# The expert bias moves from TensorE's accumulation to VectorE's residual rows

## The chip, the cores and the metric

The kernel runs on one core of a Trainium2 chip. The metric is the device time of one execution in microseconds (us); three runs of the kernel before gave 578.5, 578.75 and 578.78, a median of 578.75. The core has five engines that run side by side, each with its own queue of instructions, and that wait for each other through semaphores: TensorE (PE: matrix products; its weight loads are told apart as PEld), VectorE (DVE), ScalarE (ACT), GpSimd (POOL) and SyncE (SP, which issues most of the DMAs).

## The reference

Two layers of attention and feed-forward over 32 batches of 128 tokens with 128 features. The change concerns the last part, a mixture of eight experts, of which each token takes the one with the highest gate:

```
    indices_s = jnp.argmax(gates, axis=1)
    scores = jnp.max(gates, axis=1)
    for e in range(E):
        mask = (indices_s == e).astype(x.dtype)[:, None]
        h = jax.nn.gelu(x @ w1[e] + b1[e], approximate=False)
        out = out + mask * (h @ w2[e] + b2[e])
    out = out * scores[:, None]
    ...
    x = x + _L1_ffn_ref(_layernorm(x, axis=-1), ...)
```

So a token's row of the result is x + score * (h @ w2[e] + b2[e]), with x the residual row, and score and e those of the token.

## The kernel before

The kernel goes through its stages in order: the first attention (to about 200 us), the feed-forward layer in pairs of batches (from about 202 us, with the second attention beginning in its later pairs), the second attention (to about 474 us), and the expert stage (to about 569 us, then the last write-outs).

During the second attention, each token's normalised row, its residual row, its score and its number are scattered to a table in memory, sorted by expert. The expert stage takes 39 blocks of 128 rows from this table, each of a single expert. Three sets of buffers (`TURNS = 3`) go round. `block_loop` unrolls the first steps (block numbers up to 5), runs the next 30 in a loop of five passes with six steps each, in which the block number j is a register, and unrolls the last three. Each engine has its own copy of that loop. For block j:

- SyncE (lines 469 to 480) reads the block's first row number from memory into a register and issues two loads: XA, the normalised rows (once the buffer's previous rows are transposed), and XB, the residual rows with score and number (once the buffer's previous block has its result, `b_y_ready`).
- VectorE (lines 1743 to 1758) reads the number of the expert of block j+2 into a register (`value_load`, line 1748) and with it picks that expert's b1 (line 1749, b1e) and w1 (line 1750, W1e). Then, for block j, it waits for XB and for the buffer's last write-out, copies the row numbers (line 1754), waits for the product (`b_down`) and computes `by` = product * score + XB (line 1757).
- TensorE (lines 837 to 869) transposes XA of block j+2 (line 845), multiplies block j+1 by w1 (line 854: four products, eight matmul records), reads the expert of block j (line 860), and accumulates for block j first b2 and then h @ w2 (line 866: eight records). The b2 product at line 862 is a 16-bit matmul: `thrice`, a matrix with ones in rows 0, 32 and 64 and zeros elsewhere, against `bpieces`, which holds in those rows b2 cut into three bf16 pieces.
- ScalarE copies the transposed rows (line 1097) and applies gelu with b1 as its bias (line 1102).
- GpSimd writes `by` out, row by row, by the numbers (line 1337).

The pieces of b2 are made by VectorE in the first seven pairs of the feed-forward stage (lines 1706 to 1740, called by the pair's number from `biases`): four memsets for `thrice`, then copies and subtractions on `bpieces` and M2b, ten instructions. M2b, b2 of all experts repeated over 96 partitions, is loaded at about 190 us.

The order on each engine is that of the program; there is no planner. A wait on a semaphore stands either in the instruction that follows or in an entry of its own on the engine's sequencer, which also does the register operations.

Of the kernel before, what the change touches and what calls it, by code (L numbers as in the profile page):

```python
# [8 lines left out]
ALU = mybir.AluOpType  # L9
# [3 lines left out]
BF16 = mybir.dt.bfloat16  # L13
# [7 lines left out]
FC = FF // 128  # L21
# [39 lines left out]
def build(nc, a, out):  # L61
    ctx = ExitStack()
    with ctx:
# [10 lines left out]
        def count(value):  # L74
# [50 lines left out]
        wgr = sb("wgr", [EXPERTS, GATE])  # L125
        M1 = sb("M1", [128, EXPERTS, FF])
        M2 = sb("M2", [128, EXPERTS, FC, 128])
        M2b = sb("M2b", [96, EXPERTS, 128])
        rank = sb("rank", [128, EXPERTS])


# [48 lines left out]
        XB = [sb(f"XB{i}", [128, RW - D])[:] for i in range(TURNS)]  # L180
        bxT = [sb(f"bxT{i}", [128, 128])[:] for i in range(TURNS)]
        by = [sb(f"by{i}", [128, D + 1])[:] for i in range(TURNS)]
        bpieces = sb("bpieces", [96, EXPERTS, 128], BF16)
        b1e = [sb(f"b1e{i}", [128, FC])[:] for i in range(TURNS)]
        thrice = sb("thrice", [96, 128], BF16)
        wgT = sb("wgT", [GATE, EXPERTS])
        wgn = sb("wgn", [EXPERTS, 3])
        wgs = sb("wgs", [EXPERTS, 2, GATE])
# [53 lines left out]
        late_loads = [(F1[:], a["F1"]), (F2[:], a["F2"].rearrange("(c p) n -> p c n", p=128))]  # L242
        expert_loads = [
            (M1b[:], a["M1b"]),
            (M2b[:].rearrange("p e n -> p (e n)"), a["M2b"].rearrange("e n -> (e n)").partition_broadcast(96)),
            (M1[:], a["M1"].rearrange("e p n -> p e n")),
            (M2[:], a["M2"].rearrange("e (c p) n -> p e c n", p=128)),
        ]
# [254 lines left out]
        def _(pe):  # L503
# [334 lines left out]
            def experts():  # L838
                def step(j, r, turn):
                    n1, n2 = (r + 1) % TURNS, (r + 2) % TURNS  # L840
                    if not isinstance(j, int) or j + 2 < BLOCKS:

                        pe.wait_ge(sem(f"xa_loaded{n2}"), 16 * (turn + (r + 2) // TURNS))
                        pe.wait_ge(sem("b_xT_ready"), count(j + 2))
                        nc.tensor.transpose(bank[0][:, 0:128], XA[n2], eye[:]).then_inc(sem("b_transposed"), 1)
                    if not isinstance(j, int) or 0 <= j + 1 < BLOCKS:


                        if isinstance(j, int) and j + 2 >= BLOCKS:
                            pe.wait_ge(sem("b_xT_ready"), j + 2)  # L850

                        pe.wait_ge(sem("b_picked"), count(j + 2))
                        for c in range(FC):
                            mm = nc.tensor.matmul(bank[1 + n1][:, c * 128:(c + 1) * 128], W1e[n1][:, c * 128:(c + 1) * 128], bxT[n1],  # L854
                                                  start=True, stop=True)
                        mm.then_inc(sem("b_up"), 1)
                    if not isinstance(j, int) or 0 <= j < BLOCKS:


                        e = pe.value_load(expert[0:1, bass.ds(j, 1)], min_val=0, max_val=EXPERTS - 1)  # L860
                        pe.wait_ge(sem("b_y_ready"), count(j + 1 - TURNS))
                        nc.tensor.matmul(bank[4 + r][:, 0:D], thrice[:], bpieces[:, bass.ds(e, 1), :].rearrange("p o n -> p (o n)"),
                                         start=True, stop=False)
                        pe.wait_ge(sem("b_gelu"), count(j + 1))
                        for c in range(FC):
                            mm = nc.tensor.matmul(bank[4 + r][:, 0:D], bhT[r][:, c * 128:(c + 1) * 128],  # L866
                                                  M2[:, bass.ds(e, 1), c:c + 1, :].rearrange("p o c n -> p (o c n)"),
                                                  start=False, stop=(c == FC - 1))
                        mm.then_inc(sem("b_down"), 1)

                pe.wait_ge(sem("biases_cut"), 1)
                block_loop(pe, step, -2, BLOCKS)

            step = attention(0)
# [471 lines left out]
        def _(dve):  # L1346
# [260 lines left out]

                return step

            def ffn(early, biases):  # L1610
                def x_of(p):
                    if isinstance(p, int):
                        return lambda i: X[:, 2 * p + i, :]
                    return lambda i: X[:, bass.ds(p * 2 + i, 1), :].rearrange("p o d -> p (o d)")

                def stats_of(p, b):
                    if is_pair(p):
                        norm_stats("f_xn_ready", p, 2, x_of(p), fstats[:, b], fmv[:, b])

                def normalise(p, b):  # L1620
                    if is_pair(p):

                        dve.wait_ge(sem("f_transposed"), count(p - 1))
                        norm_apply("f_xn_ready", p, 2, x_of(p), fmv[:, b], frstd[:, b], lambda i: fxn[:, b, i, :])

                def add(p):

                    dve.wait_ge(sem("f_biased"), p + 1)
                    for h in range(2):
                        dve.wait_ge(sem("f_down"), 2 * p + h + 1)  # L1630
                        x = x_of(p)(h)
                        nc.vector.tensor_tensor(x, x, bank[(4, 7)[h]][:, 0:128], ALU.add).then_inc(sem("f_added"), 1)

                def x_stats(p):

                    dve.wait_ge(sem("f_added"), 2 * p + 2)
                    for t in range(2 * p, 2 * p + 2):
                        nc.vector.bn_stats(xst[:, t, :], X[:, t, :]).then_inc(sem("x1_stats"), 1)
                    dve.wait_ge(sem("x1_stats"), 4 * p + 2)
                    for t in range(2 * p, 2 * p + 2):  # L1640
                        nc.vector.bn_aggr(xmv[:, t, :], xst[:, t, :]).then_inc(sem("x1_stats"), 1)

                def step(p, b):
                    stats_of(p + 4, b)
                    normalise(p + 3, 1 - b)
                    if p in biases:
                        biases[p]()
                    add(p)
                    x_stats(p)
                    run_early(early, p)  # L1650

                def begin(p):

                    dve.wait_ge(sem("attn_added"), 2 * p + 2)
                    stats_of(p, p % 2)
                    if p:
                        normalise(p - 1, (p - 1) % 2)

                def rest():
                    dve.wait_ge(sem("attn_added"), B)  # L1660
                    every_pair(step)
                    dve.wait_ge(sem("f_added"), 2 * PAIRS)

                return begin, rest
# [38 lines left out]
                dve.wait_ge(sem("placing"), 13)  # L1703
                nc.vector.tensor_scalar(base[:], place[:, 2, :], float(EXPERTS * REGION), None, ALU.add).then_inc(sem("expert_ready"), 1)

            def bias_ones():

                nc.vector.memset(thrice[:], 0.0).then_inc(sem("bias_cut"), 1)
                dve.wait_ge(sem("bias_cut"), 1)
                for k in range(3):  # L1710
                    nc.vector.memset(thrice[32 * k:32 * k + 1, :], 1.0).then_inc(sem("bias_cut"), 1)

            def bias_first():

                dve.wait_ge(sem("experts_loaded"), EXPERTS_LOADED)
                nc.vector.tensor_copy(bpieces[:], M2b[:]).then_inc(sem("bias_cut"), 1)

            def bias_rest():

                dve.wait_ge(sem("bias_cut"), 5)  # L1720
                nc.vector.tensor_tensor(M2b[:], M2b[:], bpieces[:], ALU.subtract).then_inc(sem("bias_cut"), 1)

            def bias_second():

                dve.wait_ge(sem("bias_cut"), 6)
                nc.vector.tensor_copy(bpieces[32:64], M2b[32:64]).then_inc(sem("bias_cut"), 1)

            def bias_again():

                nc.vector.tensor_copy(bpieces[64:96], M2b[64:96]).then_inc(sem("bias_cut"), 1)  # L1730

            def bias_last():

                dve.wait_ge(sem("bias_cut"), 8)
                nc.vector.tensor_tensor(M2b[64:96], M2b[64:96], bpieces[64:96], ALU.subtract).then_inc(sem("bias_cut"), 1)

            def bias_third():

                dve.wait_ge(sem("bias_cut"), 9)
                nc.vector.tensor_copy(bpieces[64:96], M2b[64:96]).then_inc(sem("biases_cut"), 1)  # L1740

            def experts():
                def step(j, r, turn):
                    n2 = (r + 2) % TURNS
# [6 lines left out]
                    if not isinstance(j, int) or 0 <= j < BLOCKS:  # L1751
                        dve.wait_ge(sem(f"xb_loaded{r}"), 16 * turn)
                        dve.wait_ge(sem(f"gone_out{r}"), count(16 * (turn - 1)))
                        nc.vector.tensor_copy(by[r].bitcast(I32)[:, D:D + 1], XB[r].bitcast(I32)[:, TOKEN_AT - D:TOKEN_AT - D + 1]
                                              ).then_inc(sem("b_numbered"), 1)
                        dve.wait_ge(sem("b_down"), count(j + 1))
                        nc.vector.scalar_tensor_tensor(by[r][:, 0:D], bank[4 + r][:, 0:D], XB[r][:, SCORE_AT - D:SCORE_AT - D + 1],  # L1757
                                                       XB[r][:, 0:D], ALU.mult, ALU.add).then_inc(sem("b_y_ready"), 1)
# [112 lines left out]
            def regions_set():  # L1871
# [3 lines left out]
                nc.vector.tensor_scalar(sums[:, 0, :], rank[:], float(REGION // 128), None, ALU.mult).then_inc(sem("regions_set"), 1)  # L1875

            early = attention(1)
            begin, every = ffn(early, {0: bias_ones, 1: bias_first, 2: bias_rest, 3: bias_second, 4: bias_again, 5: bias_last,
                                      6: bias_third})
            body_loop(dve, step, START, {-3: partial(x_group, 2),  # L1880
                                         B - 8: gate_square, B - 7: mean_abs, B - 6: gate_unit, B - 5: gate_turned,
                                         B - 4: gate_plain, B - 3: gate_centred, B - 2: scale_norm, B - 1: fold_bias,
# [93 lines left out]
```

## Time and profile before

| | |
|---|---|
| median of three runs | 578.75 us |
| the three runs, lowest to highest | 578.5 to 578.78 us |
| the profiled execution: its own time is its span | 578.6 us |
| busy over the span: PE / PEld / DVE / ACT / POOL | 85 / 63 / 69 / 62 / 64% |
| expert stage, first `by` to last `by` | 491.1 to 568.9 us |
| granted clock of TensorE, mean | 0.964 |

The span runs from the first to the last instruction of one execution. Busy time counts instructions at work on an engine's data path; register operations, branches and semaphore waits of its sequencer are not counted. A letter q behind an engine's name marks such entries of its queue. "issue" as the cause of idle time means that the engine waited for nothing that the profile shows. Matmuls are pipelined, so the length of one is longer than the distance from one to the next.

### The profile page before, as it was taken

How to read it: one execution, taken by the hardware profiler on the slowest of the kernel's cores; microseconds unless marked ns; L12 is line 12 of the kernel's file. 1: busy time of each engine (PE TensorE's matmuls, PEld its weight loads, DVE VectorE, ACT ScalarE, POOL GpSimd, SP SyncE). 2: the span in 40 equal slices, each digit the busy share in tenths (PEclk: the TensorE clock that was granted, in tenths of full speed). 3: DMA queues.
4: the chain of work that ended last, by engine and by line, in shares of the span. 5: the costliest groups of instructions: out<-in, count | busy, mean ns of one | idle time of the engine just before them, and what ended most of it. 6: DMA issues, size and time to landing. Idle time of an engine off the chain costs nothing.

```text
span 578.6 us, 20130 instructions
## 1 busy us (share of the span) xinstructions
PE 493.0 (85%) x6238; PEld 361.9 (63%) x6239; DVE 399.0 (69%) x1248; ACT 357.1 (62%) x872; POOL 372.8 (64%) x755
## 2 busy tenths in 40 slices
PE   3587899999997799988999999999998834999993
PEld 2455666666665599976455555555554423999992
DVE  6687777777888578645578888888888762444441
ACT  4356677777766555653566776777765643666661
POOL 6868766676772367676556688888885561455552
PEclk9879999999999999999899999999999965999997
DMA  6664353534332860004433545444543114333330
GB/s 170 159 135 110 88 131 81 127 88 114 104 76 56 265 156 1 2 19 126 110 91 94 127 128 143 106 111 130 146 121 93 36 68 134 94 91 98 101 87 27
DMA packets 102161, 59.92 MB, mean 104 GB/s; under 512 B 20338, under 2 KB 98178, under 8 KB 102098
## 3 DMA queue, kind: packets, MB, share of 16 engines
q1 hardware_dynamic: 98738, 51.79, 35.5%
q0 software_dynamic: 2784, 6.82, 3.4%
q8 instruction: 32, 0.52, 0.4%
q10 hardware_dynamic: 576, 0.53, 0.3%
q14 instruction: 31, 0.25, 0.2%
HBM read 19.90 MB, written 8.81 MB: 50 GB/s over the span
## 4 chain that ended last, share of the span: by engine, by line
PE 47%; DVE 14%; issue 13%; SPq 8%; DMA 7%; POOL 5%; ACT 4%; ACTq 1%; DVEq 0%; POOLq 0%
DVE negmax L1448 6%; PE bank L688 6%; PE score L632 4%; PE bank L802 4%; PE scoreT L792 4%; DMA stack<-pieces 3%; PE bank L866 3%; PE bank L575 3%; PE bank L544 3%; SPq L404 3%; PE bank L703 2%; PE scoreT L854 2%; PE scoreT L661 2%; PE score L601 2%; SPq L470 2%
## 5 line engine op out<-in xcount | busy, mean ns | idle before, releaser
L1448 DVE TENSOR_REDUCE negmax<-score 128x8 f32<-128x1024 f32 x128 | 156.2, 1220 | 29.9 <-PE score L632 20.1
L975 ACT ACTIVATE P<-scoreT 128x1024 f32<-128x1024 f32 x128 | 131.0, 1024 | 40.1 <-PE scoreT L652 20.3
L688 PE MATMUL bank<-P,Vc 128*32 128x128 f32 x2048 | 82.7, 279 | 2.3 <-DVE product L1556 1.2
L632 PE MATMUL score<-stack 64*128 64x128 bf16 x1024 | 62.3, 221 | 15.6 <-DVE negmax L1448 9.5
L1337 POOL DMA_INDIRECT out<-by x39 | 40.2, 1031 | 51.3 <-issue 26.8
L632 PEld LDWEIGHTS score<-stack 64*128 64x128 bf16 x1024 | 33.6, 95 | 42.0 <-issue 23.1
L688 PEld LDWEIGHTS bank<-P,Vc 128*32 128x32 f32 x2048 | 48.6, 109 | 16.4 <-issue 4.3
L981 ACT COPY outs<-bank 128x256 f32<-128x256 f32 x64 | 23.7, 370 | 49.2 <-PE bank L688 49.2
L1199 POOL TENSOR_TENSOR pieces<-full,pieces 128x256 bf16<-128x256 f32 x63 | 42.2, 670 | 12.8 <-ACT pieces L956 12.8
L1202 POOL TENSOR_TENSOR pieces<-rest,pieces 128x256 bf16<-128x256 f32 x63 | 43.7, 693 | 4.9
L866 PE MATMUL bank<-M,bhT 128*128 x312 | 43.5, 282 | 0.3 <-ACT bhT L1102 0.3
L1200 POOL TENSOR_TENSOR rest<-full,pieces 128x256 f32<-128x256 f32 x63 | 42.4, 673 | 0.0
L1102 ACT ACTIVATE bhT<-scoreT,b1e 128x128 f32<-128x128 f32 x104 | 29.6, 368 | 15.9 <-PE scoreT L854 14.6
L1210 POOL TENSOR_TENSOR negp<-negmax,blank 128x16 bf16<-128x16 f32 x64 | 14.3, 223 | 38.4 <-DVE negmax L1448 36.9
L866 PEld LDWEIGHTS bank<-M,bhT 128*128 128x128 f32 x312 | 37.9, 192 | 1.3 <-issue 0.7
L1256 POOL DMA_INDIRECT expert_rows<-XR,sloti x32 | 32.9, 1027 | 8.8 <-issue 6.7
L1188 POOL TENSOR_TENSOR full<-rotA,rotB 128x256 f32<-128x256 f32 x31 | 22.5, 727 | 22.4 <-DVE rotB L1400 22.4
L1757 DVE SCALAR_TENSOR_TENSOR by<-bank,XB 128x128 f32<-128x128 f32 x39 | 13.7, 351 | 27.7 <-PE bank L866 20.3
L1457 DVE RECIPROCAL rden<-bank 128x16 f32<-128x16 f32 x64 | 16.2, 254 | 23.9 <-PE bank L703 23.7
L802 PEld LDWEIGHTS bank<-F,hT 128*128 128x128 f32 x256 | 31.0, 192 | 0.8
L802 PE MATMUL bank<-F,hT 128*128 128x128 f32 x256 | 31.2, 275 | 0.0
L1013 ACT ACTIVATE xn<-XR,xsh,xrs 128x128 f32 (+1 forms) x64 | 28.0, 487 | 5.2 <-POOL xsh L1162 5.1
(219 smaller groups left out, 1261.7 us busy)
## 6 DMA issues: line engine op xcount, KB each, us to landing
stack<-pieces SPq DMA_DIRECT2D x192, 128.0 KB, 2.5
ctxT<-in_ctxT SPq DMA_DIRECT2D x32, 128.0 KB, 2.4
XB<-expert_rows SPq DMA_DIRECT2D x39, 66.0 KB
XA<-expert_rows SPq DMA_DIRECT2D x39, 64.0 KB
XR<-in_x SPq DMA_DIRECT2D x4, 512.0 KB, 4.3
stack<-blank SPq DMA_DIRECT2D x32, 64.0 KB, 2.1
stack<-negpT SPq DMA_DIRECT2D x64, 32.0 KB, 1.9
M<-in_M SPq DMA_DIRECT2D x1, 2048.0 KB, 9.8
```

Of the source, the lines that this page charges most:

```text
L632: mm = nc.tensor.matmul(SCORE[:, r, i * 128:(i + 1) * 128], Qs[pb][rows, h, tb * S:(tb + 1) * S], Ks[pb][rows, kv, tb * S:(tb + 1) * S], s ...
L688: mm = nc.tensor.matmul(PVOUT[VCOL * i:VCOL * (i + 1), half * 128:(half + 1) * 128], Vc[:, k % BODY, at:at + VCOL], P32[:, c, i * 128:(i + ...
L802: mm = nc.tensor.matmul(bank[(4, 7)[h]][:, 0:128], hT[:, b, c, h * S:(h + 1) * S], F2[:, c, :], start=(c == 0), stop=(c == FC - 1))
L866: mm = nc.tensor.matmul(bank[4 + r][:, 0:D], bhT[r][:, c * 128:(c + 1) * 128], M2[:, bass.ds(e, 1), c:c + 1, :].rearrange("p o c n -> p (o ...
L975: nc.scalar.activation(P32[:, half * 2:half * 2 + 2, :], SCORET[:], ACT.Exp, scale=SCALE).then_inc(sem("exp_done"), 1)
L1102: ins = nc.scalar.activation(bhT[n1][:, c * 128:(c + 1) * 128], bank[1 + n1][:, c * 128:(c + 1) * 128], ACT.Gelu, bias=b1e[n1][:, c:c + 1])
L1199: nc.gpsimd.tensor_tensor(pc[:, 1, :], f, h, ALU.subtract).then_inc(sem(f"{nm}_pieces"), 1)
L1200: nc.gpsimd.tensor_tensor(r, f, h, ALU.subtract).then_inc(sem(f"{nm}_pieces"), 1)
L1202: nc.gpsimd.tensor_tensor(pc[:, 2, :], r, pc[:, 1, :], ALU.subtract).then_inc(sem(f"{nm}_pieces"), 1)
L1256: nc.gpsimd.indirect_dma_start(out=rows_d, out_offset=bass.IndirectOffsetOnAxis(ap=sloti[:, t:t + 1], axis=0), in_=XR[:, t, :], in_offset= ...
L1337: nc.gpsimd.indirect_dma_start(out=out, out_offset=bass.IndirectOffsetOnAxis(ap=at_, axis=0), in_=by[r][:, 0:D], in_offset=None).then_inc( ...
L1448: nc.vector.tensor_reduce(negmax[:, k % 2, :, half * HQ:(half + 1) * HQ], SCORE[:].rearrange("p r (h k) -> p r h k", h=HQ), AX.X, ALU.max, ...
```

## The change

VectorE reads the expert of block j as well, computes XB = b2 * score + XB in place once the block's XB has come, and waits for that before `by`. TensorE accumulates h @ w2 alone. The pieces, the matrix of ones and their instructions are gone, and b2 is loaded over 128 partitions instead of 96.

```
-        M2b = sb("M2b", [96, EXPERTS, 128])
+        M2b = sb("M2b", [128, EXPERTS, 128])
-        bpieces = sb("bpieces", [96, EXPERTS, 128], BF16)
-        thrice = sb("thrice", [96, 128], BF16)
-            (M2b[:]..., a["M2b"].rearrange("e n -> (e n)").partition_broadcast(96)),
+            (M2b[:]..., a["M2b"].rearrange("e n -> (e n)").partition_broadcast(128)),
...
                         pe.wait_ge(sem("b_y_ready"), count(j + 1 - TURNS))
-                        nc.tensor.matmul(bank[4 + r][:, 0:D], thrice[:], bpieces[:, bass.ds(e, 1), :].rearrange("p o n -> p (o n)"),
-                                         start=True, stop=False)
                         pe.wait_ge(sem("b_gelu"), count(j + 1))
                         for c in range(FC):
                             mm = nc.tensor.matmul(bank[4 + r][:, 0:D], bhT[r][:, c * 128:(c + 1) * 128],
                                                   M2[:, bass.ds(e, 1), c:c + 1, :].rearrange("p o c n -> p (o c n)"),
-                                                  start=False, stop=(c == FC - 1))
+                                                  start=(c == 0), stop=(c == FC - 1))
...
-                pe.wait_ge(sem("biases_cut"), 1)
+                pe.wait_ge(sem("experts_loaded"), EXPERTS_LOADED)
...
                         nc.vector.tensor_copy(by[r].bitcast(I32)[:, D:D + 1], XB[r].bitcast(I32)[:, TOKEN_AT - D:TOKEN_AT - D + 1]
                                               ).then_inc(sem("b_numbered"), 1)
+                        e = dve.value_load(expert[0:1, bass.ds(j, 1)], min_val=0, max_val=EXPERTS - 1)
+                        nc.vector.scalar_tensor_tensor(XB[r][:, 0:D], M2b[:, bass.ds(e, 1), :].rearrange("p o n -> p (o n)"),
+                                                       XB[r][:, SCORE_AT - D:SCORE_AT - D + 1], XB[r][:, 0:D], ALU.mult, ALU.add
+                                                       ).then_inc(sem("b_biased"), 1)
+                        dve.wait_ge(sem("b_biased"), count(j + 1))
                         dve.wait_ge(sem("b_down"), count(j + 1))
...
-            begin, every = ffn(early, {0: bias_ones, 1: bias_first, 2: bias_rest, 3: bias_second, 4: bias_again, 5: bias_last,
-                                      6: bias_third})
+            begin, every = ffn(early)
```

The seven functions from `bias_ones` to `bias_third` are removed with their calls.

## Rows read from the trace of the kernel before

**Rows 1.** Busy time by stretch, expert stage: start:end, length, busy us (instructions), clock, DMA.

```profile
501.00:564.00 63.00, 61.92 (x548) 60.77 (x547) 29.38 (x121) 42.04 (x152) 31.66 (x31) 1.00 0.39 96
```

**Rows 2.** Timeline of VectorE: start us, length us, instruction, [idle before, releaser].

```profile
491.08 0.35 DVE L1757 SCALAR_TENSOR_TENSOR by<-bank,XB 128x128 f32<-128x128 f32 x1 [3.98 <-PE bank L866]
...
491.81 0.17 DVE L1749 COPY b1e<-M1b 128x4 f32 x1 [0.38 <-issue]
...
501.11 0.35 DVE L1757 SCALAR_TENSOR_TENSOR by<-bank,XB 128x128 f32<-128x128 f32 x1 [0.66 <-PE bank L866]
...
507.46 0.35 DVE L1757 SCALAR_TENSOR_TENSOR by<-bank,XB 128x128 f32<-128x128 f32 x1 [0.56 <-issue]
508.29 0.17 DVE L1749 COPY b1e<-M1b 128x4 f32 x1 [0.48 <-issue]
508.42 0.43 DVE L1750 COPY W1e<-M 128x512 f32 x1
508.76 0.15 DVE L1754 COPY by<-XB 128x1 int32<-128x1 int32 x1
509.47 0.35 DVE L1757 SCALAR_TENSOR_TENSOR by<-bank,XB 128x128 f32<-128x128 f32 x1 [0.56 <-issue]
...
514.62 0.22 DVE L1749 COPY b1e<-M1b 128x4 f32 x1 [0.79 <-issue]
...
563.48 0.35 DVE L1757 SCALAR_TENSOR_TENSOR by<-bank,XB 128x128 f32<-128x128 f32 x1 [0.56 <-PE bank L866]
...
568.85 0.35 DVE L1757 SCALAR_TENSOR_TENSOR by<-bank,XB 128x128 f32<-128x128 f32 x1 [1.06 <-issue]
```

**Rows 3.** Timeline of TensorE, expert stage.

```profile
510.27 0.22 PE L862 MATMUL bank<-bpieces,thrice 96*128 x1
510.33 1.11 PE L866 MATMUL bank<-M,bhT 128*128 x8
...
528.23 0.32 PE L845 MATMUL score<-eye,XA 128*128 128x128 f32 x1 [0.49 <-DMA XA<-expert_rows]
```

**Rows 4.** Chain of waits from 512 to 532 us, shares by line.

```profile
by line: issue 27.8%; SPq L470 25.1%; SPq L480 19.3%; SPq L475 18.0%; PE bank L866 4.8%; PE score L854 2.2%; DVE by L1757 1.8%; SPq L335 0.7%; PE bank L862 0.3%; SPq L479 0.2%
```

**Rows 5.** Instructions of single lines: ns min/median/max, first and last start us.

```profile
L1748 DVEq TENSOR_LOAD <-expert x39: 300/304/906, 479.1 to 563.6; - x39
...
L1753 DVEq EVENT_SEMAPHORE  x34: 21/21/21, 482.8 to 567.4; - x34
...
L1446 DVEq ALU_OP  x1: 40/40/40, 84.4 to 84.4; - x1
...
L1400 DVE TENSOR_TENSOR rotB<-bank,sinT x1: 414/414/414, 84.8 to 84.8; 128x256 f32<-128x256 f32 x1
```

**Rows 6.** Prices of VectorE instructions: by line, then two from its timeline.

```profile
L1440 DVE SCALAR_TENSOR_TENSOR mask<-adj,upper x32: 276/286/844, 255.0 to 435.6; 128x128 bf16<-128x128 int32 x32
...
L1463 DVE TENSOR_TENSOR onorm<-bank,rden x64: 290/292/294, 39.6 to 467.4; 128x128 f32<-128x128 f32 x64
...
L1750 DVE COPY W1e<-M x39: 414/427/429, 480.6 to 564.5; 128x512 f32 x39
...
472.98 0.17 DVE L1527 SCALAR_TENSOR_TENSOR cand<-lg,rank 128x16 f32<-128x16 f32 x1
473.18 0.17 DVE L1529 TENSOR_REDUCE top<-cand 128x2 f32<-128x16 f32 x1
```

**Rows 7.** Feed-forward stage: TensorE's transposes by its timeline, and one bias instruction.

```profile
205.69 0.38 PE L782 MATMUL score<-eye,fxn 128*128 128x128 f32 x2
...
228.08 0.38 PE L782 MATMUL score<-eye,fxn 128*128 128x128 f32 x2
...
235.55 0.38 PE L782 MATMUL score<-eye,fxn 128*128 128x128 f32 x2
...
211.89 1.22 DVE L1721 TENSOR_TENSOR M2b<-M2b,bpieces 96x1024 f32<-96x1024 f32 x1
```

**Rows 8.** Busy time by stretch, end of the second attention.

```profile
455.00:460.00 5.00, 3.70 (x59) 2.08 (x55) 3.56 (x15) 3.17 (x6) 1.02 (x5) 1.00 0.12 35
```

More of the change, by code:

```diff
@@ L244, in build @@
             (M1b[:], a["M1b"]),
-            (M2b[:].rearrange("p e n -> p (e n)"), a["M2b"].rearrange("e n -> (e n)").partition_broadcast(96)),
+            (M2b[:].rearrange("p e n -> p (e n)"), a["M2b"].rearrange("e n -> (e n)").partition_broadcast(128)),
             (M1[:], a["M1"].rearrange("e p n -> p e n")),
@@ L1608, in attention, with ffn @@
                 return step
-            def ffn(early, biases):
+            def ffn(early):
                 def x_of(p):
@@ L1645, in step @@
                     normalise(p + 3, 1 - b)
-                    if p in biases:
-                        biases[p]()
                     add(p)
@@ L1704, in table @@
                 nc.vector.tensor_scalar(base[:], place[:, 2, :], float(EXPERTS * REGION), None, ALU.add).then_inc(sem("expert_ready"), 1)
[L1706 to L1740, printed above, removed]
             def experts():
```

## The prediction

> **What bounds the kernel now.** I read the views in this order: busy time by stretch, to find the stage that the change touches and its fullest engine; VectorE's timeline there, instruction by instruction; TensorE's timeline; the chain of waits; and the durations by source line. In the expert stage (about 491 to 569 us) TensorE is busy 61.92 of 63 us at a granted clock of 1.00, and VectorE 29.38 [rows 1]. The reader should not conclude that VectorE is half free. Its busy time counts only what its data path does; reading a register from memory and waiting on a semaphore is done by its sequencer, and shows up as idle time "issue" ahead of the next instruction.
>
> One block of the stage takes VectorE four instructions (b1e, W1e, the row number, `by`). The two `by` at 507.46 and 509.47 are 2.01 us apart [rows 2], which is TensorE's step: 18 weight loads with their matmuls back to back. Over the five unrolled steps (491.08 to 501.11) the mean is 2.01, over the 30 steps from 501.11 to 563.48 it is 62.37/30 = 2.08 [rows 2]. The 0.07 more is SyncE: TensorE waits now and then for XA [rows 3], and the chain of waits from 512 to 532 us runs for 62% through SyncE's queue, lines 470, 475 and 480 [rows 4]. So two limits lie close together, TensorE at 2.01 and SyncE at 2.08 us a block, and VectorE is the third: its `by` sits idle 0.55 us before b_down comes.
>
> **Part 1, TensorE's bias product goes.** From its start to that of the next matmul is 0.06 us [rows 3], and its weight load takes one of 18 equal slots of the step, 2.01/18 = 0.11 us. TensorE's own step becomes 1.90. This is worth 39 x 0.11 = 4.3 us at most, and only if TensorE still set the step. In the loop SyncE's 2.08 already stands above it, so even with VectorE out of the way I would credit only the five unrolled steps and the end, some 0.5 us.
>
> **Part 2, cutting b2 into pieces goes.** The ten VectorE instructions (1.22 us the longest) lie in the feed-forward stage. TensorE repeats there every 3.73 us: 205.69 to 228.08 is six steps of 3.73 with these instructions beside them, 228.08 to 235.55 two steps of 3.73 without [rows 7]. Gain: nothing; what hides it is TensorE, and nothing takes its place. The load of M2b grows by a third (96 to 128 partitions), lands before the feed-forward stage and is first read some 290 us later: nothing.
>
> **Part 3, VectorE's new work, step by step.** Each of 39 blocks gets a second read of a register (`value_load` of expert j), a scalar_tensor_tensor on 128x128 from SBUF, and a wait on that before `by`.
>
> The read. TENSOR_LOAD takes 0.304 us [rows 5], but with the address before it, the range check and the table address behind it the whole comes to more: from the start of `by` at 507.46 to b1e at 508.29 is 0.83 us [rows 2]. That is the price of a read in the loop, counted from when the instruction in front is handed to the engine. In the unrolled steps it is 0.10 less (idle 0.38 before b1e instead of 0.48 [rows 2]).
>
> Whether it hides. The sequencer does run ahead of a queued instruction: line 1446's register operation runs at 84.4, although rotB, which stands before it in the program, starts at 84.8 [rows 5]. So it needn't wait until W1e and the row number are through: the second read begins once the row number is handed over, about 0.25 us after b1e (0.13 to W1e [rows 2], then one or two sequencer entries of 0.02 to 0.05 [rows 5] with their gaps; an estimate). It does not run ahead past `by`, whose wait holds the sequencer: `by` at 491.08 had waited 3.98, time enough for any read, and b1e still comes 0.38 after it [rows 2]. So the two reads of a step follow one another and cannot overlap.
>
> The new instruction. None like it is in the trace. The nearest with two SBUF inputs of this shape is the mask at line 1440, minimum 0.276, median 0.286, with a constant for its scalar [rows 6]. A scalar from memory adds about 0.06: `by` takes 0.35 [rows 2] where line 1463, the same shape also from PSUM, takes 0.29 [rows 6]. I take 0.34, between 0.28 and 0.36 (0.84, the mask's maximum, is a rival below).
>
> The wait. Two dependent VectorE instructions: cand at 472.98 for 0.17, the next at 473.18 [rows 6], a gap of 0.03. If the sequencer holds the wait by itself, add some 0.07; I take 0.03, up to 0.15. What is queued behind the waiting `by` is the next step's first read; POOL's write-out, SyncE's next XB and TensorE's reuse of the bank wait for `by`, each with two blocks in hand.
>
> Sum of a loop step from `by` to `by`: 0.83 + 0.25 + 0.83 + 0.34 + 0.03 = 2.28. Each pass of six steps has 0.31 more at the back edge (idle 0.79 instead of 0.48 [rows 2]) and about 0.2 more for the wait values computed in two of its steps (an estimate from entries of 0.045 to 0.06): 0.51/6 = 0.09. Together 2.37. That is above SyncE's 2.08 and TensorE's 1.90, so **VectorE becomes the bound**, and TensorE idles a fifth of each step.
>
> 30 loop steps: 30 x (2.37 - 2.08) = +8.7. Five unrolled steps: 2.28 - 0.20 = 2.08 against 2.01, +0.35. The end (563.48 to 568.85, 5.37 us, last three blocks): VectorE needs 2.2, 1.2 and 1.2 there, 4.6, since the last two pick nothing; so TensorE and ScalarE still set it and lose three bias slots, -0.3. Before the first `by` the work is hidden, as VectorE waits 4 us there. Net +8.8 us. The profiled execution spans 578.6, its runs' median is 578.75, so 0.15 lies around the span; I add to the median: **587.6 us**.
>
> A rule is to be weighed here. Row first: the mask, a VectorE instruction with two SBUF inputs, spreads from 0.276 to 0.844 in a stage where GpSimd computes [rows 6], whereas W1e, in the expert stage beside GpSimd's write-outs, keeps to 0.414 to 0.429 [rows 6]. The Trainium skill (Advanced Engine Details and Errata, GPSIMD Details) says that GpSimd shares a read and a write interface with VectorE and collides with VectorE instructions in a two-port mode or with two SBUF inputs. By that rule the new instruction could meet the write-outs; it is the third rival.
>
> **Rivals.**
> 1. VectorE does not become the bound, because most of the second read is covered. It decides once the read, the instruction and its wait cost under 0.9 us together instead of 1.2. For it: VectorE is busy under half of the stage. Against it: the sequencer's time is not in that share. SyncE then holds the loop at 2.08 and the gain is 0.5 in the unrolled steps: 578.2; if SyncE kept up as well, up to 4.3 less, 574.5. Chance 0.06, half of it beyond 0.2%.
> 2. The row number blocks the sequencer until the engine takes it: 508.76 instead of 0.25 after b1e, so 0.22 more a step, 36 x 0.22 = +8: 595.6. Against it: the run-ahead of [rows 5]. Chance 0.05.
> 3. The shared port: 0.84 in place of 0.34 on every block, 36 x 0.5 = +18: 605.6; if a third of the blocks meet it, 593.6. Against it: W1e's steady times. Chance 0.08.
> 4. TensorE's clock falls because it idles a fifth of the step. At half speed its step would be 3.8: 578.75 + 36 x 1.7 = 640. Against it: from 455 to 460 us TensorE is busy 3.70 of 5 us and the granted clock is 1.00 [rows 8]. Chance 0.02.
>
> **How the numbers follow.** The forecast has 0.79. Its own ends: short values throughout (0.28, a hand-over at 0.23, half the loop's extra) give 2.24 a step, 583; long ones (0.36, 0.15) give 2.53, about 593. Range 583.5 to 593.5, which also takes in the light case of rival 3; left out are rival 1, rivals 2 and 4, the heavy half of rival 3 and the forecast's tails, under 0.2. What a measurement can tell from no change is 0.2%, 1.2 us. Slower 0.93, within 0.2% 0.04, faster 0.03.
>
> **What would show it.** In the changed trace: 78 TENSOR_LOADs on VectorE's queue, close to 0.30 each; `by` at 2.3 to 2.4 us from the next in the loop and no longer idle for TensorE; the new instruction at 0.34; TensorE busy about 80% of the stage at clock 1.00, now waiting for W1e; SyncE gone from the chain, with VectorE's queue in its place; the feed-forward stage still at 3.73. The prediction is wrong if the step stays at or under 2.08, or if the new instruction begins less than 0.6 or more than 1.2 us after b1e.

## The result and the profile after

The changed kernel takes 591.42 us (median of four runs, 588.58 to 593.64) against 578.76 for the kernel before on the same chip: a ratio of 1.0199, 95% interval 1.0149 to 1.0249. The ratio is formed over the executions and is not the quotient of the two medians (1.0219). In a later set it was 590.96 against 580.75, ratio 1.0174 (1.0140 to 1.0208). The forecast was 587.6, range 583.5 to 593.5: the sign and the range hold, the middle was 3.8 us low.

The profiled execution spans 590.9 us, 12.3 more than before. From the first `by` to the last, the expert stage took 77.77 us [rows 2]; it now takes 581.15 - 495.05 = 86.10, so 8.3 of the 12.3 lie in it. The other 4.0 lie ahead of it: the first `by` comes at 495.05 instead of 491.08.

VectorE's timeline of the changed kernel, answering to [rows 2] (start us, length us, instruction, [idle before, releaser]). Line 1707 is b1e, 1708 W1e, 1712 the row number, 1715 the new instruction, 1720 `by`:

```profile
495.05 0.35 DVE L1720 SCALAR_TENSOR_TENSOR by<-bank,XB 128x128 f32<-128x128 f32 x1 [3.97 <-PE bank L862]
495.80 0.17 DVE L1707 COPY b1e<-M1b 128x4 f32 x1 [0.40 <-issue]
...
506.05 0.35 DVE L1720 SCALAR_TENSOR_TENSOR by<-bank,XB 128x128 f32<-128x128 f32 x1
...
510.88 0.35 DVE L1720 SCALAR_TENSOR_TENSOR by<-bank,XB 128x128 f32<-128x128 f32 x1
511.70 0.17 DVE L1707 COPY b1e<-M1b 128x4 f32 x1 [0.48 <-issue]
511.83 0.43 DVE L1708 COPY W1e<-M 128x512 f32 x1
512.17 0.15 DVE L1712 COPY by<-XB 128x1 int32<-128x1 int32 x1
512.68 0.35 DVE L1715 SCALAR_TENSOR_TENSOR XB<-M2b,XB 128x128 f32<-128x128 f32 x1 [0.37 <-issue]
513.07 0.35 DVE L1720 SCALAR_TENSOR_TENSOR by<-bank,XB 128x128 f32<-128x128 f32 x1
...
519.84 0.35 DVE L1720 SCALAR_TENSOR_TENSOR by<-bank,XB 128x128 f32<-128x128 f32 x1
521.08 0.17 DVE L1707 COPY b1e<-M1b 128x4 f32 x1 [0.90 <-issue]
...
522.66 0.35 DVE L1720 SCALAR_TENSOR_TENSOR by<-bank,XB 128x128 f32<-128x128 f32 x1
...
575.73 0.35 DVE L1720 SCALAR_TENSOR_TENSOR by<-bank,XB 128x128 f32<-128x128 f32 x1
...
581.15 0.35 DVE L1720 SCALAR_TENSOR_TENSOR by<-bank,XB 128x128 f32<-128x128 f32 x1 [0.47 <-PE bank L862]
```

`by` at 513.07 no longer waits for TensorE: its line carries no idle time, as it follows the new instruction at once. One step is 513.07 - 510.88 = 2.19 us here; the loop's mean is (575.73 - 506.05)/30 = 2.32, against 2.08 before. The step across the back edge takes 522.66 - 519.84 = 2.82.

The chain of waits from 512 to 532 us, shares by line, and three of its pieces (start us, length us), answering to [rows 4]:

```profile
by line: issue 23.1%; DVEq L1706 22.4%; DVEq L1714 22.0%; DVE XB L1715 16.3%; DVE b1e L1707 3.2%; DVE by L1720 3.1%; DVE W1e L1708 2.7%; DVEq L1715 2.6%; DVEq L1707 2.3%; DVE by L1712 1.5%; DVEq L333 0.8%; DVEq L1711 0.4%; DVEq L1719 0.1%
...
511.96 0.31 DVEq L1714
...
512.68 0.36 DVE XB L1715
513.17 0.31 DVEq L1706
```

All that it names is VectorE's now. Lines 1706 and 1714 are the two register reads of a step, 44% together, and they are entries of the queue: none of this counts as busy. SyncE, 62% of this stretch before, is gone. The piece at 511.96 is the second TENSOR_LOAD: it starts while W1e (511.83 for 0.43) is still at work and 0.21 before the row number's copy starts. So the sequencer did run ahead of handed-over instructions.

Single lines (ns min/median/max, first and last start us), answering to [rows 5] and to the mask of [rows 6]:

```profile
L1714 DVEq FUSED_REGOPS  x49: 53/190/190, 490.3 to 579.9; - x49
L1714 DVEq TENSOR_LOAD <-expert x39: 299/303/317, 490.0 to 579.6; - x39
L1714 DVEq SEQ_ASSERT  x39: 23/23/23, 490.6 to 580.2; - x39
...
L1715 DVE SCALAR_TENSOR_TENSOR XB<-M2b,XB x39: 350/352/353, 490.7 to 580.3; 128x128 f32<-128x128 f32 x39
...
L1706 DVEq TENSOR_LOAD <-expert x39: 299/305/1171, 482.1 to 575.9; - x39
```

Busy time by stretch (start:end, length, busy us (instructions) of PE, PEld, DVE, ACT, POOL, clock, DMA), answering to [rows 1]:

```profile
501.00:564.00 63.00, 61.17 (x461) 54.18 (x461) 35.57 (x135) 37.22 (x136) 28.45 (x28) 1.00 0.34 85
```

TensorE does 461 records in the 63 us where it did 548. Its busy time hardly moves (61.17): the records of its matmuls overlap and cover a short wait. The weight loads, 60.77 us before and 54.18 now, show the slack better, as here, where they wait for W1e while the record of the transpose ahead (512.10 for 0.27) runs on past 512.31:

```profile
512.31 0.97 PEld L852 LDWEIGHTS scoreT<-bxT,W1e 128*128 128x128 f32 x8 [0.18 <-DVE W1e L1708]
```

VectorE, at 35.57 of 63 us, looks half free while it sets the pace.

### The profile page after: what moved, and what is told of

It is laid out like the page before. It is cut to its first block, busy times and chain, and to the rows that moved or that the text cites. A ratio compares the mean times of both kernels' runs of the same rounds, so it can differ in the third digit from the quotient of the medians.

```text
span 590.9 us, 20281 instructions
## 1 busy us (share of the span) xinstructions
PE 502.9 (85%) x6199; PEld 364.1 (62%) x6200; DVE 407.5 (69%) x1277; ACT 357.2 (60%) x872; POOL 370.0 (63%) x755
## 4 chain that ended last, share of the span: by engine, by line
PE 38%; DVE 18%; issue 13%; DVEq 7%; POOL 6%; SPq 6%; DMA 6%; ACT 4%; ACTq 0%; POOLq 0%
DVE negmax L1444 6%; DMA stack<-pieces 5%; PE bank L800 5%; PE bank L686 5%; SPq L402 5%; PE scoreT L790 4%; PE score L630 4%; DVEq L1714 3%; DVEq L1706 3%; PE bank L542 3%; PE bank L573 2%; DVE XB L1715 2%; PE bank L701 2%; PE scoreT L609 2%; PE score L599 2%
## 5 line engine op out<-in xcount | busy, mean ns | idle before, releaser
L862 PE MATMUL bank<-M,bhT 128*128 x312 | 44.8, 288 | 0.6 <-DVE by L1720 0.5
L852 PE MATMUL scoreT<-bxT,W1e 128*128 128x128 f32 x208 | 30.4, 291 | 1.2 <-DVE W1e L1708 1.1
```

## The experiments

Eight runs: the changed kernel once more, and seven kernels made from it or from the kernel before. The steps and stages below are worked out from the starts of `by` in each kernel's timeline of VectorE (first, sixth, thirty-sixth and last of the 39), in us:

| kernel | unrolled step | loop step | stage | median | ratio to before (95%) |
|---|---|---|---|---|---|
| before | 2.01 | 2.08 | 77.77 | 578.75 | |
| after | 2.20 | 2.32 | 86.10 | 591.42 | 1.0199 (1.0149 to 1.0249) |
| after_again | 2.20 | 2.32 | 86.03 | 590.96 | 1.0174 (1.0140 to 1.0208) |
| fixed_row | 1.89 | 2.01 | 75.07 | 580.13 | 0.9982 (0.9957 to 1.0008) |
| read_twice | 2.75 | 2.98 | 109.79 | 614.86 | 1.0579 (1.0529 to 1.0630) |
| one_read | 1.89 | 2.00 | 75.28 | 579.87 | 0.9977 (0.9951 to 1.0004) |
| no_b2 | 1.90 | 2.02 | 75.37 | 578.64 | 0.9953 (0.9924 to 0.9981) |
| sp_unrolled | 2.01 | 2.01 | 75.77 | 582.05 | 1.0003 (0.9971 to 1.0034) |
| no_b2_sp | 1.90 | 1.93 | 72.85 | 577.30 | 0.9928 (0.9893 to 0.9963) |
| one_read_unrolled | 1.89 | 1.95 | 73.29 | 577.47 | 0.9947 (0.9913 to 0.9981) |

The runs came in two groups; the kernel before had medians of 580.75 (first four) and 581.03 (last four) beside them, and the ratios are formed against those. The ratio compares whole executions, the stage column the part that the change touches.

**The changed kernel once more** (after_again, no edit).

> The changed kernel once more, beside the kernel before on the same chip. In its first profile the stage from the first to the last result of VectorE took 86.1 us instead of 77.8 (+8.3), but that stage also began 4.0 us later. My theory: the 8.3 us are the change, the 4.0 us ahead of it come from the execution (DMA times in the attention stages) and not from the change; so over five rounds the ratio comes to 1.014 to 1.016, and the profile again shows 86 us for the stage, with another start. Rival: the change also slows the stages ahead of it (by the moved buffers); then the ratio stays at 1.02 or more and the stage again begins 4 us later than 491.1.

The stage repeats to 0.07 us. The first `by` comes at 493.41, 1.6 earlier than in the first profile of the same kernel. The ratio of 1.0174 came a little over the 1.014 to 1.016 of the theory, which its interval takes in, and under the rival's 1.02. No run shows that DMA times were behind the late start; what the profiles show for it stands in the last part of the account below.

**The second read goes, the new instruction and its wait stay** (fixed_row).

```
-                        e = dve.value_load(expert[0:1, bass.ds(j, 1)], min_val=0, max_val=EXPERTS - 1)
-                        nc.vector.scalar_tensor_tensor(XB[r][:, 0:D], M2b[:, bass.ds(e, 1), :]...,
+                        nc.vector.scalar_tensor_tensor(XB[r][:, 0:D], M2b[:, 0, :],
```

> The changed kernel without the second read: every block takes the bias row of expert 0 (so the rows of other experts' biases are left out); the instruction on 128x128 and its wait stay. Theory (the register read is the price): VectorE's loop step falls from 2.32 to 0.83 + 0.13 + 0.34 + 0.13 + 0.35 + 0.04 + 0.09 = 1.91, under SyncE's 2.08, so the loop runs at 2.05 to 2.10 a block and the time is within 1.5 us of the kernel before. Rival (the instruction with two SBUF inputs and the wait on it are the price): the step stays at 2.3 or more, 587 to 591.

Its timeline of VectorE (line 1714 is the new instruction, 1719 is `by`):

```profile
511.53 0.15 DVE L1712 COPY by<-XB 128x1 int32<-128x1 int32 x1
511.59 0.34 DVE L1714 SCALAR_TENSOR_TENSOR XB<-M2b,XB 128x128 f32<-128x128 f32 x1
512.12 0.35 DVE L1719 SCALAR_TENSOR_TENSOR by<-bank,XB 128x128 f32<-128x128 f32 x1 [0.19 <-issue]
512.97 0.17 DVE L1707 COPY b1e<-M1b 128x4 f32 x1 [0.50 <-issue]
...
514.02 0.35 DVE L1719 SCALAR_TENSOR_TENSOR by<-bank,XB 128x128 f32<-128x128 f32 x1 [0.17 <-PE bank L862]
```

The new instruction starts right behind the row number, and `by` is idle before TensorE's product comes. The whole slowdown is gone, and the stage is 2.7 us shorter than before. So neither the instruction nor its wait was the price: the register read was. The loop ran at 2.01, under the 2.05 to 2.10 expected: SyncE's 2.08 was no floor (see no_b2).

**A third read, unused** (read_twice).

```
+                        dve.value_load(expert[0:1, bass.ds(j, 1)], min_val=0, max_val=EXPERTS - 1)
                         e = dve.value_load(expert[0:1, bass.ds(j, 1)], min_val=0, max_val=EXPERTS - 1)
```

> The changed kernel with the second read done twice in a row, one result unused. Theory (sequencer time adds up, nothing covers it): 0.75 to 0.83 more for each of about 37 blocks, a loop step of 3.1, 28 to 31 us over the changed kernel: 616 to 622. Rival (the reads run beside the data path and the price lies elsewhere, in the instruction or the wait): no more than 0.2 a block, at most 8 us over the changed kernel.

Its timeline of VectorE (line 1716 is the new instruction):

```profile
512.63 0.15 DVE L1712 COPY by<-XB 128x1 int32<-128x1 int32 x1
513.85 0.35 DVE L1716 SCALAR_TENSOR_TENSOR XB<-M2b,XB 128x128 f32<-128x128 f32 x1 [1.07 <-issue]
514.24 0.35 DVE L1721 SCALAR_TENSOR_TENSOR by<-bank,XB 128x128 f32<-128x128 f32 x1
```

A loop step grows by 2.98 - 2.32 = 0.66 us. That is a read by itself, without the table address that belongs to its user and without a hand-over; nothing covers it. The idle time before the new instruction grows from 0.37 to 1.07. The expected 0.75 to 0.83, and with it the step of 3.1 and the time of 616 to 622, came out a little too high (2.98, 614.86): this is the same over-priced read as in the prediction.

**The same change with one read** (one_read): block j+2's row of b2 is copied while its expert's number is in the register, two steps before it is used.

```
+        b2e = [sb(f"b2e{i}", [128, D])[:] for i in range(TURNS)]
...
                         nc.vector.tensor_copy(W1e[n2], ...).then_inc(sem("b_picked"), 1)
+                        nc.vector.tensor_copy(b2e[n2], M2b[:, bass.ds(e, 1), :]...).then_inc(sem("b_rowed"), 1)
...
-                        e = dve.value_load(expert[0:1, bass.ds(j, 1)], min_val=0, max_val=EXPERTS - 1)
-                        nc.vector.scalar_tensor_tensor(XB[r][:, 0:D], M2b[:, bass.ds(e, 1), :]...,
+                        dve.wait_ge(sem("b_rowed"), count(j + 1))
+                        nc.vector.scalar_tensor_tensor(XB[r][:, 0:D], b2e[r],
```

> The changed kernel, but the expert's bias row is copied out together with b1 and w1, where the register is already read two blocks ahead; the instruction on the residual rows takes the copy. One read a block, one more copy of 128x128. Theory: VectorE's step is 0.83 + 0.13 + 0.34 + 0.2 + 0.13 + 0.39 + 0.09 = 2.1, about SyncE's 2.08; loop step 2.08 to 2.15, time 578 to 581. Rival (any further VectorE instruction of this size costs as much as the read): 2.3 a step, 587 or more.

```profile
511.75 0.22 DVE L1710 COPY b2e<-M2b 128x128 f32 x1
511.89 0.15 DVE L1714 COPY by<-XB 128x1 int32<-128x1 int32 x1
511.95 0.34 DVE L1717 SCALAR_TENSOR_TENSOR XB<-b2e,XB 128x128 f32<-128x128 f32 x1
```

The copy takes 0.14 us of a step (from its start at 511.75 to that of the row number's at 511.89). With it in place of the read the new instruction follows the row number at once, and the stage is 75.28, 2.5 under before. The loop, at 2.00, again ran under the expected 2.08 to 2.15. The whole time can't be told from before: its interval contains 1.

**The removals alone** (no_b2): b2 is left out altogether.

```
-                        e = dve.value_load(expert[0:1, bass.ds(j, 1)], min_val=0, max_val=EXPERTS - 1)
-                        nc.vector.scalar_tensor_tensor(XB[r][:, 0:D], ...).then_inc(sem("b_biased"), 1)
-                        dve.wait_ge(sem("b_biased"), count(j + 1))
```

> The bias b2 is left out altogether: TensorE's product and the pieces are gone as in the changed kernel, and VectorE has the kernel before's four instructions and one read. It shows what the removals alone are worth, and what limits the loop then. After the runs so far (with one read a block the unrolled steps went to 1.89 and the loop to 2.00): stage 75 us, loop 2.00, as with one read, if SyncE holds the loop; 72 us and a loop of 1.90 if VectorE's remaining instruction was what held it at 2.00. Rival from the prediction (SyncE fixed at 2.08): loop 2.08, stage 77. The feed-forward stage stays at 3.73 a pair without the cutting of the pieces.

The stage is 2.4 us shorter than before, where 0.5 was credited, and the whole time is 0.9953 of that before (0.9924 to 0.9981). Why, the `by` of the kernel before show, in steps that the prediction does not show:

```profile
525.77 0.35 DVE L1757 SCALAR_TENSOR_TENSOR by<-bank,XB 128x128 f32<-128x128 f32 x1 [0.56 <-PE bank L866]
527.78 0.35 DVE L1757 SCALAR_TENSOR_TENSOR by<-bank,XB 128x128 f32<-128x128 f32 x1 [0.26 <-PE bank L866]
530.55 0.35 DVE L1757 SCALAR_TENSOR_TENSOR by<-bank,XB 128x128 f32<-128x128 f32 x1 [1.32 <-PE bank L866]
532.55 0.35 DVE L1757 SCALAR_TENSOR_TENSOR by<-bank,XB 128x128 f32<-128x128 f32 x1 [0.56 <-PE bank L866]
```

Steps of 2.01, 2.77, 2.00: the mean of 2.08 is TensorE's 2.01 with a long step now and then, not a floor. Without the bias product the same view shows:

```profile
525.64 0.35 DVE L1715 SCALAR_TENSOR_TENSOR by<-bank,XB 128x128 f32<-128x128 f32 x1 [0.45 <-PE bank L862]
527.89 0.35 DVE L1715 SCALAR_TENSOR_TENSOR by<-bank,XB 128x128 f32<-128x128 f32 x1 [0.49 <-PE bank L862]
530.11 0.35 DVE L1715 SCALAR_TENSOR_TENSOR by<-bank,XB 128x128 f32<-128x128 f32 x1 [0.78 <-PE bank L862]
532.01 0.35 DVE L1715 SCALAR_TENSOR_TENSOR by<-bank,XB 128x128 f32<-128x128 f32 x1 [0.45 <-PE bank L862]
```

The short steps take 1.89 or 1.90 (0.11 less, TensorE's slot as forecast), and two steps of 2.25 and 2.22 stand where one of 2.77 stood: part of what the slots save is given back, not nearly all of it. That it is given back to SyncE the next runs show.

**SyncE's loop written out, in the kernel before** (sp_unrolled) **and without b2** (no_b2_sp): SyncE's copy of the loop takes all its steps with numbers instead of a register.

```
-        def block_loop(eng, step, first, end):
+        def block_loop(eng, step, first, end, unrolled=False):
+            if unrolled:
+                for j in range(first, end):
+                    step(j, j % TURNS, j // TURNS + 1)
+                return
...
-            block_loop(sp, step, -TURNS, BLOCKS)
+            block_loop(sp, step, -TURNS, BLOCKS, unrolled=True)
```

> The kernel before, with SyncE's expert loop written out in 39 steps (no back edge, no second and third row read at each pass). Theory: the 0.07 a step by which the loop stands above TensorE's 2.007 come from SyncE; loop 2.01, stage 75.7 instead of 77.8, 2 us faster. Rival: they come from XA's transfers or from the other engines' back edges; loop stays at 2.06 to 2.08.

> b2 left out altogether as in the run before it, and SyncE's loop written out. Theory: with SyncE out of the way TensorE's 17 slots decide: loop 1.89, stage 72 us. Rival (another limit near 2.00, as ScalarE or the write-outs): loop 1.95 to 2.0.

In the kernel before, the loop step goes to 2.01, TensorE's own step: the 0.07 was SyncE's, as the prediction read it, and is worth 2.0 us of the stage. The whole time shows nothing of it (ratio 1.0003, interval 0.9971 to 1.0034). Its first `by` comes at 492.46, 1.4 later than in the profile of before, although nothing ahead of the stage differs but the length of SyncE's code. Without b2 the step goes to 1.93 and the stage to 72.85, between the theory (1.89 and 72) and the rival (1.95 to 2.0). What holds the remaining 0.04 a step was not traced.

**One read, with SyncE's and VectorE's loops written out** (one_read_unrolled): the edits of one_read and sp_unrolled, and the same for VectorE's loop.

> A version meant to beat both: bias row picked with b1 and w1 in the one read, and the expert loops of SyncE and VectorE written out. Theory: VectorE's step loses 0.10 for the address and its back edge, 1.9; TensorE 1.89, SyncE under it; loop 1.90 to 1.95, stage 72 to 73.5, 4 to 6 us faster than the kernel before. Rival (VectorE's data path and sequencer now hold the loop): 2.0, no better than with one read in the loop, 2.5 us.

It computes all that the reference does and beats both kernels: 0.9947 of the time before (0.9913 to 0.9981). Stage and loop step came as expected (73.29 and 1.95); of the 4 to 6 us expected of the whole time, some 3 came (1.1 to 5.1 by the interval). From 512 to 532 us its chain of waits, shares by line, is TensorE's alone:

```profile
by line: PE bank L867 49.7%; PE scoreT L857 31.6%; PE score L857 13.8%; PE score L848 5.5%; issue 0.1%
```

## Why the prediction was right, and where its sizes were off

**The mechanism held.** VectorE's sequencer became the bound, through the second register read and not through the new instruction. fixed_row and read_twice show it from both sides: take the read away and the stage is at 75.07, add one and it is at 109.79. The expert stage grew by 8.3 us where 8.8 were forecast. That the whole time of 591.42 lies inside the range is in part luck: the upper end of 593.5 was set by a step of up to 2.53 and by a light case of the shared port, neither of which came, while some 4 us came from ahead of the stage, for which the range had no term. The 0.2% (1.2 us) named as what can't be told from no change was too small as well: the intervals of the ratios reach 0.3 to 0.5% to either side. And not 0.15 but 1.8 us lie around the span (592.71 for a span of 590.9 us); the sum starts from the median and does not use this.

**The loop step, term by term**, in the step from 510.88:

| term | forecast | measured |
|---|---|---|
| `by` to b1e, the first read | 0.83 | 511.70 - 510.88 = 0.82 |
| b1e to the start of the second read | 0.25 | 511.96 - 511.70 = 0.26 |
| the second read | 0.83 | 512.68 - 511.96 = 0.72 |
| new instruction and wait, to `by` | 0.34 + 0.03 | 513.07 - 512.68 = 0.39 |
| sum | 2.28 | 2.19 |
| loop extras, mean over a pass | 0.09 | 2.32 - 2.19 = 0.13 |

The second read was mis-sized: I took 0.83 for it, which runs from `by` and so contains some 0.10 until the first TENSOR_LOAD begins; the hand-over of 0.25 counted that again. The extras were too small: the step over the back edge alone takes 0.63 more than 2.19. With 0.02 more for the new instruction, these errors leave 0.05 a step.

**The unrolled steps** came to 2.20 instead of 2.08. Three take 2.10 or 2.11, one 2.22, one 2.46. The longest, from 499.27 to 501.73, is the first block whose buffer has been used before, and its second read starts only at 500.62, when the row number's copy (500.47 for 0.15) is through: there the queue stood still as rival 2 has it (a wait ahead of the row number would do that; it was not tried).

**The end** (last three blocks) was to lose 0.3 us and took 581.15 - 575.73 = 5.42 instead of 5.37. That is wrong by 0.35, and not by VectorE's doing: in no_b2, without the new work, the end takes 567.35 - 561.98 = 5.37, so the three bias slots are worth nothing there.

**Part 1, the bias product.** The credit of 0.5 us, "in the loop SyncE's 2.08 already stands above it", was the step that failed in its reasoning. The removals are worth 2.4 us of the stage (no_b2). I took a mean over uneven steps for a limit. It had no weight in the forecast, as the new bound lies above both; had VectorE kept up, the forecast of the gain would have been too small by a factor of five.

**Part 2, the pieces.** TensorE's transposes in the feed-forward stage of the changed kernel, answering to [rows 7]:

```profile
207.21 0.38 PE L780 MATMUL score<-eye,fxn 128*128 128x128 f32 x2
...
237.06 0.38 PE L780 MATMUL score<-eye,fxn 128*128 128x128 f32 x2
```

Eight steps in 29.85 us are 3.73 each, as before: nothing gained there, as forecast.

**The rivals.** Rival 1 is out: the read is not covered. Rival 2 is out: the read starts before the row number's copy in the ordinary steps. Rival 3, the shared port, did not appear: all 39 new instructions took 350 to 353 ns with GpSimd's write-outs in the same stage. The rule of the Trainium skill (Advanced Engine Details and Errata, GPSIMD Details) has no case in this stage that bears it out. In the attention of the kernel before, one case goes its way: the longest mask of [rows 6] (0.844) starts at 255.5, beside a GpSimd instruction that runs from 255.4 for 0.804 (ns min/median/max of the instructions about 255.5):

```profile
L1440 DVE SCALAR_TENSOR_TENSOR mask<-adj,upper x2: 604/724/844, 255.0 to 255.5; 128x128 bf16<-128x128 int32 x2
```

```profile
L1233 POOL TENSOR_TENSOR XR<-XR,bias x1: 804/804/804, 255.4 to 255.4; 128x272 f32<-128x272 f32 x1
```

Another pair of masks, at 313.66, takes 0.56 for both although GpSimd is at work from 313.20 for 0.67, so the case alone shows no rule. What is shown is that the write-outs did not disturb the new instruction; no run had GpSimd compute beside it. Rival 4 is out: the granted clock is 1.00 from 501 to 564 us.

**The signs.** TensorE was to show as busy for about 80% of the stage; it shows 61.17 of 63 us. That sign was badly chosen, as said beside the busy times. By slots it is what was meant: 17 of 0.11 are 1.9 of a 2.32 step. The others came: 78 reads with medians of 0.303 and 0.305, a step of 2.32, weight loads that wait for W1e, SyncE gone from the chain; and the new instruction begins 512.68 - 511.70 = 0.98 after b1e, within the 0.6 to 1.2 that were set.

**The 3.8 us between forecast and result** don't lie in the stage, which came out 0.5 under its forecast. They lie ahead of it, as TensorE's transposes of the feed-forward stage (line 780 after, 782 before) and the row maxima of the attentions (line 1444 after, 1448 before) already show (ns min/median/max, first and last start us):

```profile
L780 PE MATMUL score<-eye,fxn x32: 272/273/328, 195.5 to 256.7; 128*128 128x128 f32 x32
...
L1444 DVE TENSOR_REDUCE negmax<-score x128: 1191/1224/1227, 21.7 to 458.6; 128x8 f32<-128x1024 f32 x128
```

```profile
L782 PE MATMUL score<-eye,fxn x32: 272/273/328, 194.0 to 255.2; 128*128 128x128 f32 x32
...
L1448 DVE TENSOR_REDUCE negmax<-score x128: 1190/1224/1226, 21.4 to 455.2; 128x8 f32<-128x1024 f32 x128
```

The transposes start 1.5 us later, before any instruction that the change touches but the load of M2b; they take the same 61.2 us; and the last row maximum starts 3.4 us later. Both pieces of lateness go with TensorE's granted clock, which is down to its lower level, 1.2 GHz, for part of two short stretches (0.54 from 276 to 280 us in the changed kernel). Busy time by stretch, laid out as for [rows 1], first after, then before:

```profile
16.00:44.00 28.00, 20.44 (x207) 13.49 (x207) 20.51 (x62) 11.43 (x26) 20.02 (x40) 0.70 0.61 148
264.00:296.00 32.00, 28.68 (x320) 17.74 (x318) 19.13 (x40) 15.56 (x35) 17.95 (x42) 0.89 0.39 97
```

```profile
16.00:44.00 28.00, 19.36 (x215) 12.73 (x215) 21.34 (x65) 11.78 (x27) 20.81 (x45) 0.82 0.61 148
264.00:296.00 32.00, 28.68 (x349) 17.12 (x347) 21.07 (x45) 15.68 (x34) 20.57 (x48) 0.95 0.41 102
```

Just before it falls TensorE is partly idle (busy 2.73 of the 4 us from 272 to 276 in the changed kernel). All ten profiles keep to the order: from the last of the transposes to the last row maximum it takes 198.4 to 199.9 us where the clock from 264 to 296 us is 1.00 (one_read, sp_unrolled, one_read_unrolled), 200.0 at 0.95 (before), 201.2 to 202.2 at 0.89 (after, after_again, fixed_row, no_b2) and 202.9 to 203.0 at 0.79 (read_twice, no_b2_sp).

What is not shown is whether the change has a part in it. For it: both profiles of the changed kernel have 0.89, and every kernel with the removals alone has 0.89 or less there, while one_read and one_read_unrolled, with the same removals and three more buffers, have 1.00 and reach their first `by` at 490.82 and 489.96, earlier than before. Against it: the whole times do not follow. Take from each ratio what its stage explains, and after_again is left with 1.8 us more than before (10.1, or 8.1 to 12.1 by its interval, for 8.3), fixed_row with 1.7 and no_b2 with 0.3 less, but one_read with 1.2 more and sp_unrolled, which has before's instructions everywhere ahead of the stage, with 2.2. So I take the lateness for spread, which is argued and not shown; up to some 4 us of a real cost ahead of the stage is not excluded.

## What to carry to other kernels

A busy share leaves out the sequencer: before putting work on a half-idle engine, lay one period of its timeline out with the "issue" gaps and ask which of them are register reads. Where a register's value is needed again later, copy what it selects while it is there: a copy that took 0.14 us of the step replaced a read of 0.72. And a mean step is no limit: look at single steps before crediting a second engine with a floor.

## What the hardware showed that was not expected

A register read on VectorE costs a step 0.66 us though its TENSOR_LOAD takes 0.30; the rest is register operations (0.19), the range check (0.02) and the gaps between these entries. At a loop's back edge the next read's b1e comes 521.08 - 519.84 = 1.24 us after `by` instead of 0.82. Writing SyncE's loop out took 2.0 us from the stage and left the whole time where it was. And a granted clock that falls for a few microseconds, far from the stage that was changed, goes with 1 to 4 us of the whole span.
